# Adding a mask and taking four row minima: two long VectorE operations in place of five short ones

## What is computed

```python
# x: (B=4, T=1024, D=256); mem_seq: (4, S=154, 256); 4 heads of 64
logits = jnp.einsum('BTKGH,BSKH->BKGTS', q, k)
masked = jnp.where(mem_mask[:, None, None, None, :], logits, MASK_FILL)
probs = jax.nn.softmax(masked, axis=-1)
enc = jnp.einsum('BKGTS,BSKH->BTKGH', probs, v)
x = x + jnp.tanh(g_xattn[0]) * (enc @ out_w)        # q, k from RMS norms of a layer norm, with rope
h = gelu(layernorm(x) @ ternary(W1).T + b1, approximate=False)
x = x + jnp.tanh(g_ffn[0]) * (h @ ternary(W2).T + b2)
```

## Time and profile before

| | before |
|---|---|
| median of 3 runs | 353.17 us (349.66 to 356.54) |
| span of the profiled execution | 350.0 us |
| PE busy | 313.3 us, 90% |
| DVE busy | 276.2 us, 79% |
| ACT busy | 235.6 us, 67% |
| POOL busy | 129.7 us, 37% |
| mean granted PE clock | 0.961 |

### The profile page before, as it was taken

The page is one execution under the profiler, slowest core; times in us unless marked ns, Lnnn a source line. Parts: engine busy times, 40 slices in busy tenths (PEclk is TensorE's granted clock), DMA queues, the critical chain, the costliest instruction groups (busy, mean ns, idle before and its releaser), DMA issues.

```text
span 350.0 us, 6845 instructions
## 1 busy us (share of the span) xinstructions
PE 313.3 (90%) x2171; PEld 288.6 (82%) x2171; DVE 276.2 (79%) x855; ACT 235.6 (67%) x595; POOL 129.7 (37%) x151
## 2 busy tenths in 40 slices
PE   8498787669799979997999979997999799999996
PEld 8387666558699969996899969996999689988976
DVE  0668799988978897889797989889798978857443
ACT  0246963299666986599658965697569865896392
POOL 7232399335313450337033612344135504350300
PEclk9789999999899989999899989998999989999999
DMA  6943000100001100110011001010011000100101
GB/s 129 274 129 121 1 2 0 63 0 3 0 2 61 61 2 0 63 61 2 0 60 45 15 0 58 11 51 0 0 63 62 1 0 3 60 2 0 47 16 62
DMA packets 12982, 13.35 MB, mean 38 GB/s; under 512 B 1780, under 2 KB 12396, under 8 KB 12956
## 3 DMA queue, kind: packets, MB, share of 16 engines
q1 hardware_dynamic: 11004, 11.52, 10.3%
q10 hardware_dynamic: 1824, 1.30, 1.5%
q0 software_dynamic: 128, 0.21, 0.7%
HBM read 8.83 MB, written 4.19 MB: 37 GB/s over the span
## 4 chain that ended last, share of the span: by engine, by line
PE 42%; DVE 18%; issue 18%; POOL 12%; ACT 6%; DMA 2%; SPq 0%; POOLq 0%; DVEq 0%; ACTq 0%
PE ps_h L919 14%; PE ps_m L919 11%; PE ps_m L1096 6%; DVE xn L647 5%; POOL prob L405 4%; PE ps_t L927 3%; POOL r L367 3%; POOL q_cos L376 3%; PE ps_s L919 3%; DVE pT_lo L652 2%; DMA w_raw<-in_ctx_tail 2%; DVE w_tern L745 1%; ACT prob L527 1%; PE ps_t L1049 1%; DVE vw_lo L728 1%
## 5 line engine op out<-in xcount | busy, mean ns | idle before, releaser
L376 POOL TENSOR_TENSOR q_cos<-q_cos,q_sin 128x256 f32<-128x256 f32 x32 | 25.9, 808 | 133.7 <-DVE q_sin L704 133.7
L919 PE MATMUL ps_h<-x1nT_hi,w_tern 128*128 128x512 f32 x128 | 58.2, 454 | 0.9 <-ACT hT_hi L556 0.9
L1096 PE MATMUL ps_m<-w_tern,hT_hi 128*128 128x256 f32 x224 | 56.8, 292 | 0.1
L919 PE MATMUL ps_h<-x1nT_lo,w_tern 128*128 128x512 f32 x128 | 54.9, 429 | 0.0
L1096 PE MATMUL ps_m<-w_tern,hT_lo 128*128 128x256 f32 x224 | 54.6, 282 | 0.0
L556 ACT ACTIVATE h_all<-ps_h,b_sb 128x512 f32<-128x512 f32 x64 | 44.1, 689 | 13.1 <-PE ps_h L919 11.6
L527 ACT ACTIVATE prob<-s_neg,s_min 128x154 f32<-128x154 f32 x128 | 52.3, 412 | 0.5 <-DVE s_min L765 0.4
L818 DVE TENSOR_TENSOR hT_lo<-h_all,hT_hi 128x512 fp32r<-128x512 f32 x64 | 41.7, 681 | 6.5 <-ACT hT_hi L556 6.5
L919 PE MATMUL ps_m<-vw_hi,pT_hi 128*128 128x256 f32 (+1 forms) x160 | 46.4, 290 | 0.3 <-DVE pT_lo L652 0.3
L405 POOL TENSOR_TENSOR prob<-prob,p_inv 128x512 f32<-128x512 f32 x32 | 33.4, 1043 | 31.8 <-DVE p_inv L769 31.8
L919 PE MATMUL ps_m<-vw_hi,pT_lo 128*128 128x256 f32 (+1 forms) x160 | 44.6, 279 | 0.0
(11 more groups left out here) (132 smaller groups left out, 830.3 us busy)
## 6 DMA issues: line engine op xcount, KB each, us to landing
x_sb<-in_x SPq DMA_DIRECT2D x8, 512.0 KB, 3.4
out_x<-x_both SPq DMA_DIRECT2D x8, 384.0 KB, 2.5
h_all<-in_w1t SPq DMA_DIRECT2D x1, 1024.0 KB, 16.5
w_raw<-in_w2t SPq DMA_DIRECT2D x1, 1024.0 KB, 5.2
out_x<-x_both SPq DMA_DIRECT2D x8, 128.0 KB, 1.7
w_raw<-in_ctx_main SPq DMA_DIRECT2D x1, 512.0 KB
wo_raw<-in_wo ACTq DMA_DIRECT2D x2, 256.0 KB, 11.1
x_both<-in_wq ACTq DMA_DIRECT2D x1, 256.0 KB, 10.9
```

The costliest lines, as they stand in the source:

```text
L376: pool.tensor_tensor(q[:], q[:], q_sin[t % 2][:], ALU.add).then_inc(q_roped, 1)
L919: m = pe.matmul(dst, lhs, rhs, start=(n == 0), stop=(n == len(pairs) - 1))
L1096: m = pe.matmul(dst, a[:, c, P * t:P * (t + 1)], w[:, c, :], start=(c == 0 and a is hT_hi), stop=(c == NF - 1 and a is hT_lo))
```

## The change

The two score banks become one PSUM tensor of two banks (`ps_both`), so that one access pattern spans both. The mask is added to all four heads by one `tensor_tensor` over 616 elements, the mask repeated by a pattern of stride 0, and one `tensor_reduce` takes the four minima. Before, head 0 was done by a `tensor_tensor` and a `tensor_reduce`, and heads 1 to 3 by a fused operation each (add and minimum in one pass, which is two instructions: the operation and a read of its accumulator). `s_first` is now signalled when all four heads are in SBUF, and PE's `scores` waits for it in place of `s_masked`.

```diff
-        ps_t, ps_m, ps_s, ps_h = psum("ps_t"), psum("ps_m"), psum("ps_s"), psum("ps_h")
+        ps_t, ps_m, ps_h = psum("ps_t"), psum("ps_m"), psum("ps_h")
+        ps_both = ctx.enter_context(nc.psum_tensor("ps_s", [P, 2, 512], F32))
+        ps_s = [ps_both[:, j, :] for j in range(2)]
...
                 def mask_and_min(t):
 
                     dve.wait_ge(s_filled, i * NT + (t + 1))
-                    s, least = s_neg[t % 2], s_min[t % 2]
-                    dve.tensor_tensor(s[:, 0, :], ps_s[0][:, 0:S], mask_now[:], ALU.add).then_inc(s_first, 1)
-                    for h in range(1, H):
-                        dve.tensor_tensor_reduce(
-                            s[:, h, :], ps_s[h // 2][:, S * (h % 2):S * (h % 2 + 1)], mask_now[:],
-                            1.0, 3.4e38, ALU.add, ALU.min, least[:, h:h + 1])
+                    s = s_neg[t % 2]
+                    bias = mask_now[:].rearrange("p (a h s) -> p a h s", a=1, h=1).to_broadcast([P, 2, HP, S])
+                    dve.tensor_tensor(s[:].rearrange("p (a h) s -> p a h s", a=2),
+                                      ps_both[:, :, 0:HP * S].rearrange("p a (h s) -> p a h s", h=HP), bias,
+                                      ALU.add).then_inc(s_first, 1)
                     dve.wait_ge(s_first, i * NT + (t + 1))
-                    dve.tensor_reduce(least[:, 0:1], s[:, 0, :], AX.X, ALU.min).then_inc(s_masked, 1)
+                    dve.tensor_reduce(s_min[t % 2][:], s[:], AX.X, ALU.min).then_inc(s_masked, 1)
...
                     if isinstance(i, int) and i == 0 and t == 0:
                         pe.wait_ge(kk_set, 4)
                     else:
-                        pe.wait_ge(s_masked, i * NT + t)
+                        pe.wait_ge(s_first, i * NT + t)
```

## The result

The changed kernel takes 356.5 us (median of 4 runs, 355.71 to 357.98) against 352.19 us of the kernel before (4 runs): a ratio of 1.0189, 95% interval 1.0104 to 1.0273. It is slower by about 2%; the interval leaves open on which side of 2%. The profiled execution took 355.75 us and has a span of 353.8 us, so 1.95 us lie around a span, and not the 3.2 us of the forecast.

The account below looks back on a forecast made before the run. Each step was taken as bound partly by PE, partly by a chain through DVE holding two of four mask_and_min. 353.2 + 6.6 (4.5 + 1.15 + 1.0) - 0.8 = 359.0 us, +1.7%; range 352.5 to 363.

Parts of the forecast that it names:

- The pair's length: On DVE: add 796 ns, wait 0.04 us, reduction 791 ns; 1.54 us start to next instruction against 1.15.
- The rival by operation count: DVE's cost goes by the number of operations: 2.9 us gained, 350.3 us; chance 0.04.
- Which tiles pay: Third and fourth tiles cost 0.75 us a step, 4.5 in steps 2 to 7; steps 0 and 1 add 2.15.
- The moved wait: PE's scores may overwrite the banks at 0.80 us instead of 1.24; worth nothing, since scores also wait for q_lo.
- The clock's term: Behind xn_T pauses PE's clock halves for 3.4 us (a fall, 1.7 us); half a fall, 0.8 us, subtracted.
- the falls go: Moved pauses no longer bring PE to 1.2 GHz behind xn_T: 353.0 us with four missing, 349.6 with six; chance 0.10.
- The base: The runs' median, 353.2 us, taken as 3.2 us above the profiled span of 350.0.
- One wait: PE's pauses: a new one of 0.4 us ahead of scores(3), and the one ahead of xn_T grows to 2.4.
- more is hidden: ACT or POOL is last between mask_and_min(3) and xn_T: 4.4 us in place of 6.6, about 357; chance 0.12.

Follow-up runs that it names:

- experiment 7: Changed kernel with its long add over both banks cut into four of 154 elements, one a head, the reduction left whole: 358.17 us.
- experiments 2 and 3: Kernel before with the new pair only in tiles 0 and 1 (354.11 us, ratio 1.0057), or only in tiles 2 and 3 (355.27 us, 1.0112).
- experiment 1: Changed kernel with PE's scores waiting for s_masked again, as before the change: 357.39 us, ratio 1.0162 to the kernel before.
- experiment 9: Kernel before with 8 unused matmuls of constants issued by PE ahead of xn_T: 343.72 us, where the kernel before has 351.42.

## Why the prediction was right

**The pair's length was right to a hundredth.** 792 and 795 ns against 796 and 791, the 0.04 us between them, 1.54 us from the add to the next instruction in both tiles. What carried this was counting from start to start, together with the choice of the add's slope for the reduction, which one size alone (307 ns) could not settle and which could have been 561 ns; the measured 795 settles it at 1.06 ns an element. Behind the count from start to start stands experiment 7: 0.07 us for an operation that is recorded with 0.31. The rival by operation count would have made the changed kernel faster, and experiment 7 slower by 0.15 us an operation. The Trainium skill's "VectorE: DVE Perf Modes" advises in "Rules for kernel authors" to minimise the number of operations. The runs agree that an operation more costs time, but its 0.07 us are small beside the 0.48 us of 462 elements at 1.05 ns.

**Which tiles pay was right.** 0.72 us a steady step against 0.75. The 0.03 between them are a slip of the sum: from the fourth add to `p_lo(0)` it was 1.21 us and the pair's own 1.54 follow, which is 0.33 more and not 0.36. Tiles 0 and 1 are free, and tiles 2 and 3 pay (experiments 2 and 3); the two parts of the program cost 4.6 and 2.1 us against 4.5 and 2.15. Which tiles of steps 0 and 1 make up the 2.1 no run isolates. The moved wait was idle (experiment 1).

**The clock's term was a guess that held.** The forecast took off half a fall, 0.8 us. The profiled execution missed two, 3.3 us, but that was a draw: the four runs had 5.6 falls on average and the kernel before 6.2, half a fall apart. Nothing in the forecast says why it should be a half, so this is luck. Of the rival "the falls go" nothing is left beyond that one execution. That a fall costs 1.6 us (1.73 by the line through the runs) was near the 1.7 reckoned.

**The base was too high.** 3.2 us were put around the span of 350.0, and 1.95 belong there, so that an execution of that profile takes 352; the median of 17 later runs is 351.9, and the first three runs' 353.2 was a draw. From the 359.0 of the forecast to the 356.5 measured, 1.3 us are this base. The other 1.2 us are a price that comes out lower in the runs' times (5.9 us) than in the traces (6.7), and the chance of four runs; the record does not part them.

**One wait was put in the wrong place.** PE was to wait 0.4 us ahead of `scores(3)` and 2.4 ahead of `xn_T`. It waits 0.30 and 2.06, and the pause ahead of `xn_T` is as long as before (2.05). In between, PE's weight load for `p_T(1)` now waits for the bank that `p_lo(0)` frees, in the weight-load rows of the changed kernel's timeline:

```profile
159.69 0.42 PEld L1050 LDWEIGHTS ps_t<-ident_sb,prob 128*128 128x128 f32 x4 [0.34 <-DVE pT_lo L654]
```

A further 0.1 us of PE's idle time and 0.3 of its weight loads lie ahead of the attention product that needs `pT_lo`. The step as a whole grows by what the chain over DVE grows. The case "more is hidden" fell: nothing but DVE, and POOL behind it, was last between the fourth tile and `xn_T`.

## What to carry to other kernels

Compare a fused operation with its unfused pair by elements passed and by the distance between starts; the recorded durations of short operations overlap, and here their sums promised a gain of 0.17 us a tile where the pair costs 0.39. Then look which of the tiles stand on the chain that feeds the waiting engine: two of four were free here, and a wait that is relaxed behind another wait for the same engine gains nothing. Where two kernels differ in something that comes and goes from run to run, as the falls do here, compare single steps with and without it, and count it in every run before one profile's count is taken as the change's doing. Before shortening what is on such a chain, look at its longest piece: moving a POOL operation away from `norm1` gave some four times what this change cost (18.4 us against 4.3).

## What the runs showed of the hardware

- A DVE `tensor_scalar` from SBUF to SBUF is held up beside POOL operations on SBUF. `norm1`'s four instructions take 4.21 us beside 1.04 + 0.41 + 2.42 us of POOL and 2.15 beside the first two. A single one of them takes 0.40 us where POOL is idle and 2.47 us beside `add_b2`'s 2.42. The adds that read PSUM keep 0.31 us beside POOL (L759 at 152.58 in the earlier trace rows, beside `normalise(0)`).
- "VectorE: DVE Perf Modes" of the Trainium skill says in "Two Vector instructions with no wait between them" that the second SBUF read interface is shared with GpSimd. The trace agrees with it in the numbers above, if that is the cause, which no run here isolates.
- Pauses of 2.05 us ahead of the same instruction were followed by a fall to 1.2 GHz in some steps and not in others of one execution; behind the pauses filled to 0.28 to 0.44 us in the profiled execution of experiment 9 none came. The runs of the kernel before spread over 4%, from one fall to nine.
- A matmul of fp32 constants with 128 columns is two records in the trace and keeps PE for 0.22 us (28 records of 14 matmuls in 3.1 us from first to following start).
- Fp32 adds and reductions of 154 elements take 312 and 307 ns, those of 616 elements 792 and 795: both cost 1.04 to 1.06 ns an element, and independent ones start 0.22 to 0.24 us apart at 154 elements.
